# Pre-norm state-space block and top-1 mixture of experts: first layer norm on ScalarE, router fed with raw rows

## What is computed

```python
x = L0_attn_x                                   # (2, 4096, 512) f32
x = x + attn(layernorm(x), ...)                 # layernorm: (x - mean) / sqrt(var + 1e-5), no gain
x = x + ffn(layernorm(x), gate_w, expert_w)

def attn(x, ...):
    s  = sigmoid(silu(x @ s_w1.T + s_b1) @ s_w2.T + s_b2)
    u  = (x @ B_w.T + B_b) * s                  # 128 states
    hs = scan over t of  h = h @ A.T + u_t
    y  = hs @ C_w.T + C_b + x @ D_w.T + D_b
    return y * sigmoid(x @ g_w.T + g_b)

def ffn(x, gate_w, expert_w):                   # 8 experts of 512 x 512
    chosen = argmax(x @ gate_w.T)               # one expert for each token
    return x + x @ expert_w[chosen].T
```

## Time and profile before

| what | value |
|---|---|
| time, median of 3 runs | 1120.49 us (1078.44 to 1120.79) |
| the profiled execution: span from first to last instruction | 1120.9 us |
| TensorE products busy | 1002.2 us, 89% |
| VectorE busy | 931.3 us, 83% |
| GpSimd busy | 550.0 us, 49% |
| ScalarE busy | 265.0 us, 24% |
| mean granted TensorE clock | 0.986 of full |
| 16 blocks | about 0 to 781 us |
| experts' weights and last router | about 781 to 830 us |
| 71 slots | about 830 to 1121 us |

### The profile page before, as it was taken

How to read it: one execution, slowest core, us unless ns; L and a number is a source line. 1 busy time by engine, 2 the same in 40 slices (tenths; PEclk the granted TensorE clock), 3 DMA queues, 4 the chain that set the end, 5 groups by cost and what they waited for, 6 DMA issues and landing times. The chain is left out here.

```text
span 1120.9 us, 17697 instructions
## 1 busy us (share of the span) xinstructions
PE 1002.2 (89%) x5009; PEld 782.3 (70%) x5010; DVE 931.3 (83%) x1875; ACT 265.0 (24%) x470; POOL 550.0 (49%) x597
## 2 busy tenths in 40 slices
PE   8898989999899998989999899999558888888996
PEld 7676867778677776867777677776446666566785
DVE  6788898988989888898988989889878788788653
ACT  5132221213222132221213222222531111111110
POOL 1244454534534453454534545354656555565675
PEclk9999999999999999999999999999789999999998
DMA  8041212112111222201112021200554333343342
GB/s 298 1 160 39 76 38 75 57 63 106 37 75 37 75 75 75 75 37 75 53 61 111 37 75 37 75 38 37 202 193 132 116 128 124 121 132 119 128 147 69
DMA packets 47289, 101.22 MB, mean 90 GB/s; under 512 B 5781, under 2 KB 6549, under 8 KB 47264
## 3 DMA queue, kind: packets, MB, share of 16 engines
q1 hardware_dynamic: 33680, 61.93, 16.7%
q0 software_dynamic: 10800, 33.70, 7.8%
q10 hardware_dynamic: 2784, 5.31, 1.4%
HBM read 64.85 MB, written 37.90 MB: 92 GB/s over the span
## 5 line engine op out<-in xcount | busy, mean ns | idle before, releaser
L434 POOL TENSOR_TENSOR gated_bias<-gate,y_bias 128x512 f32<-128x512 f32 x64 | 86.6, 1353 | 160.5 <-ACT gate L551 153.8
L1338 PE MATMUL y<-expert_hi,x1T_hi 128*128 x284 | 119.3, 420 | 18.1 <-issue 11.7
L488 POOL DMA_INDIRECT out<-gate,ids x71 | 71.2, 1003 | 114.2 <-issue 103.7
L1003 DVE TENSOR_SCALAR x_norm<-x_rows 128x512 f32<-128x512 f32 x71 | 122.8, 1730 | 0.0
L1338 PE MATMUL y<-expert_lo,x1T_hi 128*128 x284 | 112.2, 395 | 0.0
L1338 PE MATMUL y<-expert_hi,x1T_lo 128*128 x284 | 112.0, 394 | 0.0
L1055 PE MATMUL gates<-GwT_hi,xT_hi 128*128 128x512 f32 x256 | 106.2, 415 | 0.0
L1055 PE MATMUL y<-DwT_hi,xT_hi 128*128 128x512 f32 x256 | 104.3, 407 | 0.5 <-DVE gateT L664 0.5
L1057 PE MATMUL y<-DwT_hi,xT_lo 128*128 128x512 f32 x256 | 100.8, 394 | 0.0
L1056 PE MATMUL gates<-GwT_lo,xT_hi 128*128 128x512 f32 x256 | 100.7, 393 | 0.0
L1056 PE MATMUL y<-DwT_lo,xT_hi 128*128 128x512 f32 x256 | 100.4, 392 | 0.0
(11 more groups left out here) (227 smaller groups left out, 2444.1 us busy)
## 6 DMA issues: line engine op xcount, KB each, us to landing
x_rows<-routed_rows SPq DMA_DIRECT2D x71, 258.0 KB, 2.6
x_in<-L_attn_x SPq DMA_DIRECT2D x32, 512.0 KB, 4.0
x_rows<-L_attn_x SPq DMA_DIRECT2D x32, 512.0 KB, 3.9
raw_weights<-L_ffn_expert_w ACTq DMA_DIRECT2D x5, 1024.0 KB, 6.3
raw_weights<-L_ffn_expert_w SPq DMA_DIRECT2D x3, 1024.0 KB, 10.4
routed_rows<-padrow SPq DMA_DIRECT2D x9, 258.0 KB, 3.0
out<-gate,ids POOLq DMA_INDIRECT x71, 2.8
raw_weights<-L_attn_D_w SPq DMA_DIRECT2D x1, 1024.0 KB, 7.4
```

The lines of the kernel that those rows point to most:

```text
L434: nc.gpsimd.tensor_tensor(gbias[i % 2][:], gate[:, i, :], bias_y[:], ALU.mult).then_inc(S_["bias_gated"], 1)
L488: nc.gpsimd.indirect_dma_start(out=out_rows, out_offset=bass.IndirectOffsetOnAxis(ap=ids[m][:, 0:1], axis=0), in_=res[m], in_offset=None, ...
L1003: nc.vector.tensor_scalar(rnorm[m], rows[m][:, 0:D], rows[m][:, MEAN:MEAN + 1], rows[m][:, RSTD:RSTD + 1], ALU.subtract, ALU.mult).then_in ...
L1338: ins = nc.tensor.matmul(Y[m % 2][:], x2T[a][:, k, m % 2 * P:(m % 2 + 1) * P], flat[w][:, bass.ds(first + k * D, D)], start=(k == 0 and a ...
```

## The change

- The first layer norm of blocks 1 to 15 goes from VectorE to ScalarE, as an activation `Identity(rstd * x + shift)` with shift = -mean * rstd. GpSimd makes the shift with two more small instructions for each block, right behind the reciprocal root and ahead of the block's gate bias work. Block 0 keeps VectorE.
- On ScalarE these four activations stand: two behind the sigmoid of gate 1, one behind the sigmoid of gate 2, one behind the rounding of the states (hT_hi). The sigmoid of gate 2 is moved ahead of hT_hi.
- The router takes the raw rows x1 instead of normalised ones (the scale of a row doesn't change which score is the greatest), with router weights from which each expert's mean is taken once at the start (three VectorE instructions, `centre_gate`). `normalise2` goes away; TensorE's turns of the router wait for the added rows (x1_ready).
- TensorE's loop is written for two blocks at a time, since the buffer of x1 rows is now part of the instruction.

The diff, cut to its core (left out: names of semaphores, and the three other calls of tail_turn, which change as the one shown):

```diff
@@ -99,6 +99,8 @@
         mv1, mv2 = kb("ln1_mean_var", [P, NT, 2]), kb("ln2_mean_var", [P, NT, 2])
+        neg1, shift1 = kb("ln1_minus_mean", [P, NT]), kb("ln1_shift", [P, NT])
+        gstat, gmean = kb("gate_w_stats", [E, 6]), kb("gate_w_mean", [E, 2])
         ve1, ve2 = kb("ln1_var_eps", [P, NT]), kb("ln2_var_eps", [P, NT])
@@ -212,7 +214,7 @@
         JOB_LOAD = ([(S_["s1_loaded"], 16)] * KD + [(raw_loaded[0], RAW_NEED[0])] * 2
-                    + [(raw_loaded[r], RAW_NEED[r]) for r in (1, 2) for _ in range(KD)] + [(S_["aux_loaded"], 32)] * 2)
+                    + [(raw_loaded[r], RAW_NEED[r]) for r in (1, 2) for _ in range(KD)] + [(S_["aux_loaded"], 32), (S_["gate_centred"], 1)])
@@ -396,6 +398,10 @@
                 nc.gpsimd.tensor_tensor(rs1[:], ve1[:], mhalf[:], ALU.pow).then_inc(S_["rstd1_ready"], 1)
+                counted_waits(pool, (S_["shift1_ready"], b))
+                nc.gpsimd.tensor_scalar(neg1[:], mv1[:, :, 0], -1.0, None, ALU.mult).then_inc(S_["neg1_ready"], 1)
+                counted_waits(pool, (S_["neg1_ready"], b + 1), (S_["rstd1_ready"], b + 1))
+                nc.gpsimd.tensor_tensor(shift1[:], neg1[:], rs1[:], ALU.mult).then_inc(S_["shift1_ready"], 1)
@@ -550,8 +556,16 @@
+            def normalise1(b, i):
+
+                act.wait_ge(S_["shift1_ready"], b + 1)
+                act.wait_ge(S_["xT_psum"], NT * b)
+                nc.scalar.activation(xn[:, i, :], xin[:, i, :], ACT.Identity, bias=shift1[:, i:i + 1],
+                                     scale=rs1[:, i:i + 1]).then_inc(S_["xn_ready"], 1)
+
             def body(b):
                 tail = not (isinstance(b, int) and b == 0)
+                ahead = not (isinstance(b, int) and b == LASTB)
                 for i in range(NT):
@@ -583,15 +597,23 @@
                 gates(b, 1)
+                if ahead:
+                    normalise1(b + 1, 0)
+                    normalise1(b + 1, 1)
+                gates(b, 2)
+                if ahead:
+                    normalise1(b + 1, 2)
                 act.wait_ge(S_["h_sum"], b + 1)
                 nc.scalar.activation(token_order(hT[0]), z[:], ACT.Copy).then_inc(S_["h_hi"], 1)
-                gates(b, 2)
+                if ahead:
+                    normalise1(b + 1, 3)
                 gates(b, 3)
...
             body(1)
-            with act.Fori(2, NBLK) as b:
+            with act.Fori(2, LASTB) as b:
                 body(b)
+            body(LASTB)
@@ -637,16 +659,15 @@
-                counted_waits(dve, (S_["stats1"], NT * (b + 1)), (S_["rstd1_ready"], b))
+                counted_waits(dve, (S_["stats1"], NT * (b + 1)), (S_["rstd1_ready"], b), (S_["neg1_ready"], b))
                 for i in range(NT):
...
-            def normalise1(b, first=0, end=NT):
-                dve.wait_ge(S_["rstd1_ready"], b + 1)
-                dve.wait_ge(S_["mv1_ready"], b + 1)
-                wait(dve, S_["xT_psum"], NT * b)
-                for i in range(first, end):
+            def normalise_first():
+                dve.wait_ge(S_["rstd1_ready"], 1)
+                dve.wait_ge(S_["mv1_ready"], 1)
+                for i in range(NT):
                     nc.vector.tensor_scalar(xn[:, i, :], xin[:, i, :], mv1[:, i, 0:1], rs1[:, i:i + 1],
@@ -658,10 +679,20 @@
                     if n == 3:
-                        normalise1(0)
+                        normalise_first()
                     dve.wait_ge(S_["w_hi"], n + 1)
...
                     nc.vector.tensor_tensor(lo, job_view(n), hi.bitcast(f32), ALU.subtract).then_inc(S_["w_lo"], 1)
+
+            def centre_gate():
+
+                dve.wait_ge(S_["aux_loaded"], 32)
+                nc.vector.bn_stats(gstat[:], raw_gate).then_inc(S_["gate_stats"], 1)
+                dve.wait_ge(S_["gate_stats"], 1)
+                nc.vector.bn_aggr(gmean[:], gstat[:]).then_inc(S_["gate_mean"], 1)
+                dve.wait_ge(S_["gate_mean"], 1)
+                nc.vector.tensor_scalar(raw_gate, raw_gate, gmean[:, 0:1], None, ALU.subtract
+                                        ).then_inc(S_["gate_centred"], 1)
@@ -731,15 +762,6 @@
                 ins.then_inc(S_["mv2_ready"], 1)
-
-            def normalise2(b, q, first=0, end=NT):
-                dve.wait_ge(S_["rstd2_ready"], b + 1)
-                dve.wait_ge(S_["mean_copied"], b + 1)
-                wait(dve, S_["x2T_psum"], NT * b)
-                for i in range(first, end):
-                    nc.vector.tensor_scalar(xn2[:, i, :], xrow[q][:, i, 0:D], xrow[q][:, i, MEAN:MEAN + 1],
-                                            xrow[q][:, i, RSTD:RSTD + 1], ALU.subtract, ALU.mult
-                                            ).then_inc(S_["xn2_ready"], 1)
@@ -854,6 +876,7 @@
                     nc.vector.tensor_tensor(bias_y[:], bias_y[:], bias_c[:], ALU.add).then_inc(S_["bias_sum"], 1)
+                    centre_gate()
                 if ahead and tail:
@@ -878,8 +901,6 @@
                     ln1_stats(b + 1, 3)
-                if tail:
-                    normalise2(old, oldq, 0, 1)
@@ -897,15 +918,12 @@
                 if tail:
-                    normalise2(old, oldq, 1, 2)
                     tail_lo(old, 0)
...
                 to_pairs(b)
-                if tail:
-                    normalise2(old, oldq, 2, 3)
-                else:
+                if not tail:
                     ln1_stats(b + 1, 2)
@@ -916,7 +934,6 @@
                     tail_lo(old, 2)
-                    normalise2(old, oldq, 3, 4)
                 over(b, 2)
@@ -927,14 +944,10 @@
                 gate_sum(b, 1)
-                if ahead:
-                    normalise1(b + 1, 0, 1)
-                else:
+                if not ahead:
                     list_gaps()
                 over(b, 5)
-                if ahead:
-                    normalise1(b + 1, 1, 2)
-                else:
+                if not ahead:
                     slot_experts(0, FIRST)
@@ -946,7 +959,6 @@
                 if ahead:
-                    normalise1(b + 1, 2, NT)
                     if tail:
@@ -984,7 +996,6 @@
             experts(0, E_STEPS[0])
-            normalise2(LASTB, 1)
             for pair in range(2):
@@ -1111,15 +1122,15 @@
-            def tail_turn(b, i):
-                pe.wait_ge(S_["xn2_ready"], NT * b + i + 1)
+            def tail_turn(b, q, i):
+                pe.wait_ge(S_["x1_ready"], NT * b + i + 1)
                 bank = turn_bank(b, i)
...
                 for k in range(KD):
-                    ins = nc.tensor.transpose(bank[:, k * P:(k + 1) * P], xn2[:, i, k * P:(k + 1) * P], ident[:])
+                    ins = nc.tensor.transpose(bank[:, k * P:(k + 1) * P], xrow[q][:, i, k * P:(k + 1) * P], ident[:])
                 ins.then_inc(S_["x2T_psum"], 1)
@@ -1233,7 +1244,7 @@
                 if tail:
-                    tail_turn(b - 1, 0)
+                    tail_turn(b - 1, 1 - q, 0)
                 y_dense(b, 1, 2)
@@ -1279,10 +1290,11 @@
-            body(0)
-            body(1)
-            with pe.Fori(2, NBLK) as b:
-                body(b)
+            body(0, 0)
+            body(1, 1)
+            with pe.Fori(1, NBLK // 2) as t:
+                body(t * 2, 0)
+                body(t * 2 + 1, 1)
@@ -1305,12 +1317,12 @@
             experts(0, E_STEPS[0])
-            tail_turn(LASTB, 0)
-            tail_turn(LASTB, 1)
+            tail_turn(LASTB, 1, 0)
+            tail_turn(LASTB, 1, 1)
             experts(E_STEPS[0], E_STEPS[1])
             tail_scores(LASTB, 0)
-            tail_turn(LASTB, 2)
-            tail_turn(LASTB, 3)
+            tail_turn(LASTB, 1, 2)
+            tail_turn(LASTB, 1, 3)
             tail_back(LASTB, 0)
```

More of the change, by code:

```diff
@@ L162, in preln_ssm_moe_kernel @@
                      "bias_sum w_turned w_hi w_lo pow_psum pow_copied pow_hi pow_lo "
-                     "stats1 mv1_ready ve1_ready rstd1_ready xn_ready xT_psum xT_hi xT_lo "
+                     "gate_stats gate_mean gate_centred stats1 mv1_ready ve1_ready rstd1_ready neg1_ready shift1_ready xn_ready xT_psum xT_hi xT_lo "
                      "s1_psum s1_sig silu_ready silu_hi silu_lo bt_psum s2_psum sel_ready "
@@ L166, in preln_ssm_moe_kernel @@
                      "g_psum g_sum gate_ready bias_gated biased y_psum yg_ready x1_ready "
-                     "stats2 mv2_ready ve2_ready rstd2_ready mean_copied xn2_ready x2T_psum x2T_hi x2T_lo "
+                     "stats2 mv2_ready ve2_ready rstd2_ready mean_copied x2T_psum x2T_hi x2T_lo "
                      "scoresT_psum scoresT_ready scores_psum scores_ready top_ready sig_warm hit_ready cand_ready best_ready bounded_ready onehot_ready "
@@ L1187, in down, with body @@
                 pairs(b, NSTEP, S_["down_psum"])
-            def body(b):
+            def body(b, q):
                 tail = not (isinstance(b, int) and b == 0)
@@ L1243, in body @@
                 if tail:
-                    tail_turn(b - 1, 1)
+                    tail_turn(b - 1, 1 - q, 1)
                 to_chunks(b)
```

(4 more changed lines are left out.)

## The result

The changed kernel takes 1107.88 us (median of 4 runs, 1106.04 to 1111.48); the kernel before, in the same session, 1120.27 us (median of 4, 1078.44 to 1120.79). Medians over all runs give 1107.88 / 1120.27 = 0.989, 1.1% less. Set against the one run of before in which the slots fell into their short form (1078.44 us, explained with the experiments), the kernel after, whose slots were in the long form each time, is 2.8% slower (2.3 to 3.2%). My 1095 us was 12.9 us too low. The result lies inside my range, but not in the case that I held likeliest, faster by over 2%.

A forecast was written before the change was run, and what follows sets the result against it. TensorE, 89% busy, was taken as the bound, with at most 4.2 us of a 47.93 us block lost to VectorE, held up by GpSimd. 1120.9 - 21 + 0.7 + 1.2 - 6.5 = 1095.3 us; range 1060 to 1112.

The forecast's parts named there:

- 14 blocks: Steady blocks: each 1.3 to 1.7 us shorter, taken as 1.5, so 21 us off in all.
- block 0: Start-up: the three centre_gate instructions on VectorE lie in the weight-splitting chain, up to 1.4 us, partly covered; +0.7 us.
- block 15 and the tail: Block 15's choose is caught under GpSimd, +1.2 us; behind it x1 is turned sooner and slot_place falls earlier, 6.5 us off.
- slots: Slot loop behind the blocks: code untouched, change from slow to fast phase stays where it was, so no change in time.
- Over(b, 3): Scan in a block: VectorE's cast and remainder fit ahead of GpSimd's later multiply, so TensorE issues 1.6 us sooner.
- over(b, 4): Next scan level: VectorE's cast meets GpSimd's later add, so the next scan product gives back 0.65 us.
- choose caught: End of block: choose runs under GpSimd's multiply and add, two exposed steps wait, TensorE stands still 1.4 to 1.9 us.
- hT_lo behind the ranks: End of block: next block's product with the states comes 2.85 us behind the ranks instead of 4.65, via hT_lo.
- The two ends of the prediction: Gain of 1.3 or 1.7 us a block, the two outcomes of is_top's start against GpSimd's multiply.
- the race that I named: End of block: start of is_top against GpSimd's multiply, 0.1 us apart, decides between the two ends of the block's gain.
- Slower, by the clock: Rival: TensorE's clock differs and the kernel gets slower, reckoned with 2.8 us a block; chance 0.08.
- Little gain, 1107 to 1117: Rival: slow slot phase lasts to the end (1117 us), or block 15's end gives nothing and races are lost (1107); chance 0.14.

The follow-up runs named there:

- the slots kept apart: Either kernel with GpSimd's add of a slot's rows waiting for VectorE's normalisation of the next slot: kernel before 1071.40 us, changed kernel 1059.93 us.
- all three edits: Changed kernel plus GpSimd's longer wait in the slots, 50 idle VectorE instructions at the start, gate 2's sigmoid back behind the cast of hT_hi: 1042.12 us.

## Why the prediction was wrong

Against the spans, 1120.9 and 1109.6:

| term | forecast | measured |
|---|---|---|
| 14 blocks | -21 | -5.2 |
| block 0 | +0.7 | +1.0 |
| block 15 and the tail | +1.2 - 6.5 | -7.3 |
| slots | 0 | +0.2 |
| sum | -25.6 | -11.3 |

- *Over(b, 3), over(b, 4), choose caught, hT_lo behind the ranks*: right, each within 0.1 us where it can be read, and the undisturbed block is 46.25 us for 46.4.
- *Who waits for GpSimd*: which steps of `choose` under a GpSimd instruction wait was my estimate, from the two steps of the earlier trace rows and the cast and remainder of the earlier trace rows; the runs show single steps and no rule. In block 9 best<-candidate ran inside GpSimd's add and took 0.19 us (436.66), while is_top and best_bounded took 1.31 and 0.90. The two ends of the prediction are there (ten blocks with two steps caught, four with 0.4 us more), but not by the race that I named: the multiply started 0.04 us ahead of is_top in all of them, and they differ in whether candidate is caught (1.30 or 1.31 us; by the times in the trace the add starts 7 or 8 ns ahead of it) or not (0.19 us; 2 to 4 ns ahead).
- *"14 blocks x 1.5 = 21 us"* is the step that failed. It took one block for all fourteen. VectorE's own instruction stream was no term of the sum: I counted what the removed instructions take and who waits for them, not where they leave the loop. Five jumps back cost 48.7 to 49.3 less 46.25, some 2.7 us each, 13.5 us in sum; between the medians with the slots kept apart it is 11.5.
- *Slower, by the clock*: it is there, and 0.08 was too little for it. My 2.8 us a block was an estimate from the first slot product before, where TensorE had stood idle, the granted clock was 0.55 and 12 products took 5.11 us for 3.04; no run shows 2.8. It takes 1.6 us where it strikes, and it struck three blocks of the profiled run on their own (4.6 us with the 47.5 of block 14). Against it I had that the 1.5 us wait before left products at 0.36 to 0.40 us. That is right for waits of that length: the clock is 1.00 for 3 us behind this one of 1.47 us, and behind none of the waits of 1.34 to 1.37 us does it fall. It said nothing of the 1.74 us that my own range of 1.4 to 1.9 us held, and only behind those did the clock fall. The stall's 13.5, these 4.6 and 0.2 us of block 2, less 14 times the 0.18 us by which the undisturbed block beat its forecast (46.25 for 46.43), are the 15.8 us that the blocks are short.
- *The tail*: right in size. The stuck instruction changed its name, and GpSimd's row of pieces still costs 6 us (is_top takes 6.48 us).
- *Little gain, 1107 to 1117*: the time came out there, for neither of the reasons that I gave it.
- *Slots*: their two forms were read rightly as the reason for 1078.44, though a late slot takes 3.2 us from start to start, not 3.15. That a wait of one slot more removes the long form, and with it more than the whole change brings, I did not see.

## What to carry to other kernels

A change that removes instructions from an engine with a loop also moves the loop. In the runs here that can cost 2.2 to 2.9 us at a jump back for a body of 292 instructions and 2.9 to 3.2 us for one of 321, in some places and not in others. For a loop of such a size, look in the trace for idle time on "issue" behind the jump back, and at the packets of the instruction queue, before believing any sum made from one iteration; and read two iterations in a row, not one. When a kernel has two times, find what keeps the longer one going before comparing small changes: here it was one GpSimd add on top of one VectorE normalisation, and it was worth 48 to 50 us.

## What I had not expected of the hardware

- A jump back in the stalled place leaves VectorE idle for 2.2 to 2.9 us in the changed kernel and 2.9 to 3.2 us in the kernel before, and in the changed kernel for 0.9 to 1.2 us again two instructions on (the [0.93 <-issue] above). That this is the fetching of code is read from the packets of the instruction queue, 39 to 41 for 14 or 15.
- 0.07 to 0.09 us for an instruction that only waits on semaphores that are fulfilled: 40 of them 2.7 and 3.0 us, 60 of them 4.7, 200 of them 18.6.
- The granted clock falls behind none of 51 waits of 1.34 to 1.37 us and behind 24 of 47 waits of 1.73 to 1.76 us, unevenly from run to run; the times of one kernel then differ by up to 10 us (1048.40 to 1058.86).
- The collision in the slots is stable: in the profiled runs of both kernels it lasts until about 1030 to 1043 us, though nothing in the code asks for it. The normalisation of 0.54 us ends 0.30 us behind an add of 1.28 us. But by the profile it starts 0.77 us ahead of that add, enough to be done before it; why it is held all the same stays open. The scatter beside it (905.21) does not hold it, since with the same scatter and no add it takes 0.54 us (902.23).

The best version found, 1042.12 us, is the changed kernel with all three edits, 7% below the kernel before at 1120 to 1122 us.
